# Column hats of the last image: their second step moved from ScalarE to VectorE

## What is computed

```python
py = yg[None, None, None, :, None] + ky[None, None, :, None, None] + dy
px = xg[None, None, None, None, :] + kx[None, None, :, None, None] + dx
...
val = corner(y0i, x0i, (1 - ly) * (1 - lx)) + corner(y0i, x0i + 1, (1 - ly) * lx) + corner(y0i + 1, x0i, ly * (1 - lx)) + corner(y0i + 1, x0i + 1, ly * lx)
val = val * mask[:, :, None]
return jnp.einsum('bgckhw,ogck->bohw', val, wr) + b_dcn[None, :, None, None]
```

## Time and profile before

| | |
|---|---|
| median of 3 runs | 13684.42 us (13674.05 to 13690.25) |
| the profiled execution | 13709.62 us, its span 13707.8 us |
| busy over the span | PE 10759.4 us (78%), DVE 9356.9 (68%), ACT 8473.2 (62%), POOL 7025.2 (51%) |
| L1571 DVE weigh | 4032 of 0.819 us |
| L1237 ACT column_hats | 4032 of 0.623 us |
| L1233 ACT column_distances | 4032 of 0.711 us |
| L686 POOL first sum of a group | 1344 of 1.830 us |
| mean granted TensorE clock | 0.905 |

### The profile page before, as it was taken

The page is one execution under the profiler, slowest core; times in us unless marked ns, Lnnn a source line. Parts: engine busy times, 40 slices in busy tenths (PEclk is TensorE's granted clock), DMA queues, the critical chain, the costliest instruction groups (busy, mean ns, idle before and its releaser), DMA issues.

```text
span 13707.8 us, 498669 instructions
## 1 busy us (share of the span) xinstructions
PE 10759.4 (78%) x187900; PEld 8101.4 (59%) x187900; DVE 9356.9 (68%) x13829; ACT 8473.2 (62%) x17364; POOL 7025.2 (51%) x6167
## 2 busy tenths in 40 slices
PE   3678888888888888888888888888888888842888
PEld 2356666666666666666666666666666666631666
DVE  6558776776767677676767767676776767732854
ACT  1356666666666666666666666666666666631676
POOL 0035555545455554545555454555545454566467
PEclk8789999999999999999999999999999999976998
DMA  4244444445444444544444454444444444421444
GB/s 129 58 98 116 116 116 119 116 108 121 112 114 117 114 117 108 122 113 115 114 119 117 106 124 111 114 116 120 117 112 120 110 116 117 116 65 37 108 127 111
DMA packets 1847018, 1516.69 MB, mean 111 GB/s; under 512 B 1006688, under 2 KB 1381984, under 8 KB 1841568
## 3 DMA queue, kind: packets, MB, share of 16 engines
q1 hardware_dynamic: 1834468, 1474.31, 43.3%
q0 software_dynamic: 9216, 2.38, 0.2%
HBM read 1297.68 MB, written 178.25 MB: 108 GB/s over the span
## 4 chain that ended last, share of the span: by engine, by line
issue 33%; PE 21%; POOLq 18%; POOL 8%; DVEq 6%; DVE 5%; ACT 5%; SPq 2%; DMA 1%; ACTq 0%
POOLq L687 10%; POOLq L689 6%; PE windows L1024 4%; PE bank_small L982 4%; PE bank_small L1035 3%; DVEq L1509 3%; DVEq L1458 2%; POOL gbuf L758 2%; POOL wy L678 2%; PE windows L998 2%; PE bank_scores L901 1%; POOL val L691 1%; DVE ol L1510 1%; PE bank_post L955 1%; POOL prod L686 1%
## 5 line engine op out<-in xcount | busy, mean ns | idle before, releaser
L1571 DVE TENSOR_TENSOR prod<-windows,wy 128x640 f32<-128x640 f32 x4032 | 3294.9, 819 | 2345.9 <-PE windows L998 1642.4
L686 POOL TENSOR_TENSOR prod<-prod 128x768 f32<-128x768 f32 x1344 | 2459.8, 1830 | 3697.7 <-DVE prod L1571 3691.0
L1024 PE MATMUL windows<-fx,hats 64*64 64x80 f32 x129024 | 3317.1, 243 | 355.3 <-DVE valt L1560 123.4
L1024 PEld LDWEIGHTS windows<-fx,hats 64*64 64x64 f32 x129024 | 2662.2, 139 | 1578.2 <-issue 1492.8
L1233 ACT ACTIVATE hats<-hats,cst 128x512 f32<-128x512 f32 x4032 | 2867.5, 711 | 85.4 <-DMA hats<-sample_columns 51.7
L1510 DVE SCALAR_TENSOR_TENSOR ol<-xpad,lepw,ol 128x448 f32<-128x448 f32 x2688 | 2701.7, 1005 | 248.7 <-issue 17.2
L1237 ACT ACTIVATE hats<-hats 128x512 f32<-128x512 f32 x4032 | 2511.5, 623 | 21.3
L688 POOL TENSOR_TENSOR prod<-prod 128x384 f32<-128x384 f32 x1344 | 1588.5, 1182 | 198.0 <-issue 6.8
L982 PE MATMUL bank_small<-wom,ofp 128*128 128x216 f32 x8064 | 1642.6, 360 | 0.0
L1182 ACT ACTIVATE pr<-bank_scores,nmx 128x256 f32<-128x256 f32 x1568 | 656.4, 470 | 1509.4 <-DVE nmx L1488 1509.3
L691 POOL TENSOR_TENSOR val<-prod 128x384 f32<-128x384 f32 x1344 | 1407.4, 1047 | 270.1 <-issue 232.8
(11 more groups left out here) (193 smaller groups left out, 13176.2 us busy)
## 6 DMA issues: line engine op xcount, KB each, us to landing
hats<-sample_columns SPq DMA_DIRECT2D x2688, 336.0 KB
ksel<-k_windows SPq DMA_DIRECT2D x3136, 32.0 KB
vsel<-v_windows SPq DMA_DIRECT2D x3136, 32.0 KB
fx<-map_columns SPq DMA_DIRECT2D x64, 420.0 KB
xpad<-in_x SPq DMA_DIRECT2D x17, 1568.0 KB, 11.3
q_windows<-qb SPq DMA_DIRECT2D x112, 224.0 KB, 3.0
k_windows<-kb SPq DMA_DIRECT2D x112, 224.0 KB, 3.2
v_windows<-vb SPq DMA_DIRECT2D x112, 224.0 KB, 3.2
```

The source lines that it names most:

```text
L686: pool.tensor_tensor(v[:, :, 0:n], v[:, :, 0:n], v[:, :, n:2 * n], ALU.add)
L1024: last[h] = pe.matmul(o[m], hat[:, m], fx[XP * h:XP * h + XP, g, row:row + WR, :].rearrange("p r c -> p (r c)"), start=True, stop=True)
L1571: dve.tensor_tensor(o, x, w.unsqueeze(3).to_broadcast([128, 2, CP * WR, CG]), ALU.mult).then_inc(s_wm, 1)
```

## The change

In `body(None, NIMG - 1)` ScalarE leaves `column_hats` out, and VectorE does it: after weighing slot q (and copying turned samples, where the slot has them) it waits for the distances of the chunk three slots ahead and computes max(0, -d + 1) in place, with two TENSOR_SCALAR operations and a drain between them. The semaphore that TensorE waits for (s_hat) is incremented by VectorE's second operation in place of ScalarE's. In all other bodies nothing changes.

```diff
@@ scalar, body
-                        if hi is not None:
+                        if hi is not None and xi is not None:
                             column_hats(hi, hg, q % CPG)
@@ vector
+            def column_hats(i, n, c):
+
+                dve.wait_ge(s_cab, cnt(i, NT * Q, n * CPG + c + 1))
+                v = hats[:, n % HR, c * CP:(c + 1) * CP, :].rearrange("p j n -> p (j n)")
+                dve.tensor_scalar(v, v, -1.0, 1.0, ALU.mult, ALU.add)
+                dve.drain()
+                dve.tensor_scalar(v, v, 0.0, None, ALU.max).then_inc(s_hat, 1)
@@ vector, body
                             weigh(di, t, q)
                             if bi is not None:
                                 copy_samples(bi, bt, p, hb[n % 2])
+                        hi, hg = group_of(di, xi, t * NG + q // CPG + 1)
+                        if hi is not None and xi is None:
+                            column_hats(hi, hg, q % CPG)
```

## The result

The median after is 13849.8 us (13831.3 to 13862.8, 4 runs) against 13680.6 before (4 runs): a ratio of 1.0122, interval 1.0105 to 1.014, so 169 us or 1.2% slower. The forecast was 13845 us, +160. The profiled execution after took 13842.6 us, its span 13840.8.

A forecast was written before the change was run, and what follows sets the result against it. GpSimd was taken to bound the last image at 18.46 us a tile. VectorE's pairs, blocked behind its sums, make that 24.4: 5.9 us over 27 tile intervals, +160 us on 13684.4, so 13845 us, range 13735 to 13935.

The forecast's parts named there:

- GpSimd sets the pace before: Last image: GpSimd's three sums, drains and the gap behind L707 hold the whole chain of waits, 18.46 us a tile.
- Taking the ACTIVATEs away: ScalarE, last image: 249 ACTIVATEs of 0.622 us, 155 us in all, beside the chain; worth nothing in time.
- The price of one operation: VectorE's 128x512 TENSOR_SCALAR: 0.53 us by interpolation, ends 0.49 and 0.82; a pair alone 1.14 us.
- The blocking: A VectorE TENSOR_SCALAR meeting a GpSimd sum at SBUF ends 0.25 us behind that sum; its partner meets the next.
- The walk: One tile stepped through, wN weighing N, hN the pair after it: period 24.4 us; +110 to +210 us has chance 0.60.
- The new wait and the flag: VectorE's slot 4 hats wait for ScalarE's distances, 2.5 us behind L774; the L1553 flag, deform and slot 6's windows follow.
- The waits of L686: Sign in the profile after: GpSimd's L686 waits for VectorE's weighing L1571 once a tile, about 3.7 us.
- The low clock: TensorE's deform (L1035) takes 3.60 us instead of 2.17 at its low clock; period then 25.7 us.
- rival (b): Low clock in most tiles (1.3 us) plus sums delayed (2.2 us): period 27.9, +255 us, 13940; above +210 has shared chance 0.13.
- (a): Rival: VectorE never blocked at the port, only new wait and own fullness: 2.1 us a tile, +60 us, 13745; chance 0.19.
- (c): Rival: the pairs are hidden in VectorE's idle time, 18.3 under 18.46 us a tile; within 27 us of 13684; chance 0.05.
- (d): Rival: fewer ScalarE instructions make every GpSimd gap short and VectorE keeps up: saves 42 us, 13642; chance 0.03.

The follow-up runs named there:

- run 6: Kernel before, ScalarE making all hats; VectorE only waits after each weighing of the last image for the distances three slots ahead: 13662.7 against 13682.4 us, ratio 0.9985.
- run 9: Kernel before; in the last image TensorE runs deform ahead of the turns and VectorE writes the flag at the start of slot 4: 13679.3 us, ratio 0.9991.
- run 8: Kernel before; in the last image VectorE takes row distances (L672), row weights (L678) and mask bound (L667) from GpSimd: 13643.2 us, ratio 0.9975.
- run 7: Changed kernel with pairs replaced by copies from PSUM (second hats step left out) and the flag written ahead of weighing 4, last image: 13665.0 us, ratio 0.9991.
- run 1: Changed kernel with each TENSOR_SCALAR pair replaced by two 128x256 COPYs out of PSUM, second hats step left out: 13724.6 against 13689.3 us, ratio 1.0026.
- run 5: Changed kernel with the flag written at the start of slot 4, ahead of weighing 4, in the last image: 13811.8 us, ratio 1.01.
- run 12: Kernel with VectorE making one chunk's hats in three, flag moved into slot 3 ahead of the pair: 13687.7 against 13685.6 us before, ratio 1.0006.
- run 4: Changed kernel, but VectorE makes only the hats in slots 0, 3 and 6 (83 pairs instead of 249), ScalarE the others: 13725.4 us, ratio 1.0035.
- run 2: Changed kernel with the pair's intermediate value in an unused PSUM bank, same result: 13841.9 us, ratio 1.0115.

## Why the prediction was right, and where two terms cancelled

**GpSimd sets the pace before.** Shown: runs 6 and 9, which touch the other chains, stay within 20 us, and run 8, which shortens GpSimd's, gains. Not all of its engine time counts, though: L672 runs beside the jump (run 8).

**Taking the ACTIVATEs away is worth nothing.** In line with run 7: with the pairs' cost hidden and ScalarE relieved, the time is that of before.

**The price of one operation** was a mis-sized term: 0.53 us by interpolation, 0.419 and 0.428 measured, a free pair 0.92 us and not 1.14. The sources were TENSOR_SCALARs with a strided input and column operands, and that they would carry over was my choice. The row of the Trainium skill (VectorE: DVE Perf Modes, section on the errata) that the prediction used gave an estimate of 0.33, nearly as far off on the other side. The same section of the Trainium skill adds that this row is too low for the duration of a single operation and that the measured fixed part is about 150 cycles; in place of the 58 that makes an estimate of 0.42 us, and the trace agrees, with 0.419 and 0.428.

**The blocking** was right in mechanism and place. The walk had h2's second half, both of h5 and h8 and the first of h0 blocked, and so they are in nearly all of the 28 tiles. Of h3 it had both; the first half found its sum nearly over (a median of 0.49 us). The mean is 0.82 us where 0.87 was said; the longest is 1.94, where over 2 was said. Run 1 sizes it: 119 us by the stretch, 134 by the medians.

**The new wait and the flag.** The wait was counted as one of two causes; run 6 shows that alone it is none. What costs is the flag behind pairs that do work, blocked (run 5) or not (run 7 against run 1). The walk gave it nothing in the 24.4 ("under h5"), and w6 waited 1.3 us a tile. Run 5 sizes it: 31 us by the stretch, 40 by the medians.

**The waits of L686** were to come once a tile. They come in all three groups, 0.6, 1.7 and 4.8 us a tile. The walk's own times hold the second: group 0 and L678 are done at 13.9, and group 1 can't start before w5 ends at 16.2. The list of signs left it out.

**The low clock** was put aside for the likely case and kept for rival (b). It is the rule after, not the exception: L1035 by line, ns of one matmul, in the 24 tiles after and before.

```profile
L1035 PE MATMUL bank_small<-valt,wdcn x432: 274/421/553, 13176.9 to 13746.9; 128*128 128x128 f32 x144
```

```profile
L1035 PE MATMUL bank_small<-valt,wdcn x434: 273/275/422, 13204.3 to 13647.0; 128*128 128x128 f32 x145
```

275 and 421 ns are the same matmul at the 2.4 and at the 1.2 GHz level. Of the matmuls recorded, 373 of 432 took over 0.4 us after and 168 of 434 before. So the sign that was to speak for (b) came, and (b)'s time didn't: of its two terms only the clock's 1.3 us is there, while L686 takes 1.86 us on average for 1.83, L688 and L691 as before. The mean granted clock of the rows by stretch fell from 0.91 to 0.77; TensorE had waited for the flag just before deform. That wait alone doesn't set the level: in run 5 it is gone, and the median is 421 ns still. What does set it isn't shown, nor what the low clock alone costs.

So two terms were off in opposite directions: operations that were 0.11 us cheaper, nine free halves a tile or 1.0 us (the walk leaves ten free, but h2's first only lengthens the wait of its second), against a slow deform that the walk priced at 1.3. The period came out at 24.6 for 24.4, and the sum at 171 for 160. That the sum lay so near is luck: the total was better than its parts deserved.

**Rivals.** (a) is run 1: 13725 for the 13745 worked out. (c) failed only by the blocking and the flag, run 7. (d) did not happen, but half of its premise did: after, each of 25 gaps behind L707 was short (L667 found GpSimd idle for 2.2 to 2.5 us, against 2.2 to 5.6 before). It bought nothing, since VectorE was 4.3 us late.

## What to carry to other kernels

An engine's idle share doesn't say that work fits into it: ask which of its operations share an access path with the engine that sets the pace. Here a short operation that met a long one there cost the rest of the long one, twice for a pair, and a version three fifths longer each that avoids the path can be as fast. Look at what stands behind the inserted work in the same stream; moving a 0.14 us flag that another engine waits for took away a loss of 36 us (run 12 against run 4). Look at the granted clock after the change too. And before pricing what an engine is relieved of, check that it doesn't run beside something longer on the same engine, and that a wait in the list isn't a jump under another name.

## What the runs showed of the hardware

A TENSOR_SCALAR of 128x512 f32 from SBUF to SBUF takes 0.42 us free of GpSimd, and 0.68 us with a PSUM operand. Behind a GpSimd sum it ended 0.28 us after the sum's end. GpSimd pays too, less: L686 starting 0.16 us into a pair's first half took 1.93 us for 1.82, and L667, met by TENSOR_SCALARs, a median of 0.62 for 0.38.

GpSimd's gap behind L707, the same instructions each time, lasted 2.4 to 5.8 us in the kernel before and up to 5.7 in run 8, and stayed near 2.5 in the changed kernel and in runs 4 and 5, where GpSimd waited for VectorE 3 us a tile and more. That is no rule: in run 2 GpSimd waited 4.8 us a tile for VectorE, and the gap was 4.5 us on average. What the long gaps are made of stays open: no run changes the gap by itself. It matters for reading the small differences here, since in runs 6 and 12 a gap 1.2 to 1.5 us shorter hides 0.8 to 1.3 us a tile of waiting.
